# Graph attention with eight heads on one core: the value product visited once per step, and a head's output summed on ScalarE and GpSimd in the second head group

## What is computed

```python
h = jnp.maximum(_layernorm(x, axis=-1), 0.0)
adj = jnp.maximum(adj, eye)
q, k, v = (einsum('nd,hdk->hnk', h, W) for W in (Wqs, Wks, Wvs))
scores = einsum('hqk,hmk->hqm', q, k) * 64 ** -0.5
scores = scores + 0.01 * eye - 1e16 * (1.0 - adj)
att = softmax(scores, axis=-1)
return x + einsum('hqm,hmk,hko->qo', att, v, Wo)
```

## Time and profile before

| | |
|---|---|
| runs of the kernel | 2651.34 us median of 3 (2651.14 to 2653.06) |
| the profiled execution | 2648.64 us, of which 2647.1 us from its first to its last instruction |
| PE | busy 98% of the span, clock 0.998 of full speed |
| DVE | busy 85% |
| ACT | busy 70% |
| POOL | busy 48%, half of it issuing the moves |

### The profile page before, as it was taken

One profiled execution on the slowest core, in us unless ns is written; L12 is line 12 of the kernel. 1 busy time (PEld: TensorE's weight loads), 2 busy tenths in 40 slices (PEclk: granted clock), 3 DMA queues, 4 the chain that ended last, 5 costly groups with the idle time before them and its releaser, 6 DMA issues.

```text
span 2647.1 us, 58489 instructions
## 1 busy us (share of the span) xinstructions
PE 2597.6 (98%) x17344; PEld 1897.9 (72%) x17344; DVE 2254.0 (85%) x3833; ACT 1844.7 (70%) x3041; POOL 1281.6 (48%) x2424
## 2 busy tenths in 40 slices
PE   8999999999999999999999999999999999999997
PEld 5777777777777777777767777777777777777775
DVE  8888888888888888888858888888888888888885
ACT  5677676776767767777747677777767777776764
POOL 3355655556566555665403444434343444434343
PEclk9999999999999999999999999999999999999999
DMA  7467777677778767787645556666555666655563
GB/s 187 125 166 169 182 177 181 171 166 173 174 177 192 171 167 166 172 181 176 162 137 126 138 144 152 165 145 161 144 138 145 153 161 147 162 141 140 144 145 105
DMA packets 268608, 419.06 MB, mean 158 GB/s; under 512 B 100544, under 2 KB 121536, under 8 KB 268544
## 3 DMA queue, kind: packets, MB, share of 16 engines
q1 hardware_dynamic: 178784, 231.24, 34.3%
q0 software_dynamic: 89760, 187.05, 30.8%
HBM read 136.84 MB, written 46.27 MB: 69 GB/s over the span
## 4 chain that ended last, share of the span: by engine, by line
PE 85%; SPq 5%; DMA 4%; DVE 3%; issue 2%; POOL 0%; ACT 0%; DVEq 0%; POOLq 0%; ACTq 0%
PE psS L511 31%; PE psO L548 16%; PE psT L524 15%; PE psO L534 15%; SPq L301 5%; DMA S<-S 3%; PE psS L181 2%; DVE S L777 2%; PE psP L496 2%; PE psP L165 2%; PE psP L484 1%; DVE S L798 1%; PE psO L484 1%; DMA rden_scratch<-rden 0%; POOL S L362 0%
## 5 line engine op out<-in xcount | busy, mean ns | idle before, releaser
L362 POOL DMA_DIRECT2D S<-S x2048 | 1005.6, 499 | 1098.2 <-DVE S L798 1047.3
L777 DVE CUSTOM_DVE_ANT_0 S<-psS,B 128x1024 f32<-128x1024 f32 x1024 | 1227.5, 1218 | 217.8 <-PE psS L511 149.2
L662 ACT ACTIVATE S<-S,negm 128x1024 f32<-128x1024 f32 (+1 forms) x768 | 1095.9, 1428 | 43.9 <-DVE negm L784 43.5
L669 ACT ACTIVATE PT<-psT 128x512 f32<-128x512 f32 x1024 | 594.8, 595 | 254.0 <-PE psT L524 235.3
L511 PE MATMUL psS<-K,QH 128*128 128x512 f32 x2048 | 724.8, 435 | 16.9 <-DVE mx L777 16.4
L511 PE MATMUL psS<-K,QL 128*128 128x512 f32 x2048 | 640.5, 394 | 0.0
L798 DVE STREAM_TRANSPOSE S<-S 128x2048 f32<-128x2048 f32 x256 | 590.4, 2306 | 38.7 <-PE psO L548 35.2
L524 PEld LDWEIGHTS psT<-ident,S 128*128 128x128 f32 x4096 | 480.5, 140 | 185.9 <-issue 73.1
L524 PE MATMUL psT<-ident,S 128*128 128x128 f32 x4096 | 606.6, 276 | 2.9 <-ACT PT L669 2.9
L534 PE MATMUL psO<-PT,V 128*64 128x256 f32 x4096 | 492.1, 382 | 0.0
L548 PE MATMUL psO<-S,V 128*64 128x256 f32 x4096 | 470.3, 382 | 2.4 <-DMA S<-S 2.4
(11 more groups left out here) (51 smaller groups left out, 968.4 us busy)
## 6 DMA issues: line engine op xcount, KB each, us to landing
S<-S SPq DMA_DIRECT2D x2048, 64.0 KB, 3.0
S<-S POOLq DMA_DIRECT2D x2048, 64.0 KB, 2.8
B<-in_adj POOLq DMA_DIRECT2D x128, 256.0 KB, 6.8
bias_scratch<-B SPq DMA_DIRECT2D x64, 512.0 KB, 3.8
B<-bias_scratch SPq DMA_DIRECT2D x128, 256.0 KB, 4.3
hq<-hT_scratch SPq DMA_DIRECT2D x32, 256.0 KB, 4.8
RB<-rden_scratch SPq DMA_DIRECT2D x128, 64.0 KB, 3.4
S<-in_x SPq DMA_DIRECT2D x8, 512.0 KB, 4.6
```

The lines of the kernel that those rows point to most:

```text
L362: pool.dma_start(dst, src).then_inc(late_sent[q][half], 16)
L662: nc.scalar.activation(part, part, ACT.Exp, bias=negm[:, h % 2, q:q + 1], accum_out=sums[:, h % 2, q, e:e + 1]).then_inc(probs_ready, 1)
L669: nc.scalar.activation(PT[:, s % RING, :], psT[s % 2][:, :], ACT.Copy).then_inc(pt_act, 1)
L777: nc.vector.tensor_tensor_reduce(out=part, in0=psS[j % 2][:, :], in1=B[:, q, k * SLOT:(k + 1) * SLOT], scale=SCALE, scalar=LOWEST, op0=ALU ...
```

## The change

- On PE all eight slots are transposed before any value product. The three runs of value products (slots 0 to 3, late keys, slots 4 to 7), which stood in two places of a step, follow each other in one place, after score 7 of the next step and ahead of score 0 of the step after it.
- So that eight slots can wait for their product, slots 4 to 7 are taken into a part of `S` that has already been transposed (`PT_of`).
- On DVE the row's end (`row_done`) is cut off from mask 3 and mask 7; the first stands behind mask 4. `denominators` stands ahead of masks 6 and 7, `transpose_late` of q 1 and `add_heads` stand ahead of masks 0 and 1.
- On ACT the exponentials are in another order; the third piece of q 0 comes last in the step, behind the copy of `psO`.
- In group two, ACT copies both halves of `psO` (after a wait for `projected`), and POOL adds and scales them (`sum_and_scale`), behind its moves of the step; DVE's `sum_halves` is used in group one alone.
- POOL waits for other semaphores ahead of the next group's loads.

```diff
+EXP_ORDER = [(0, 0), (0, 1), (1, 0), (1, 1), (0, 2), (1, 2)]
...
+    def PT_of(h, s):
+        if s < RING:
+            return PT[:, s, :]
+        first = (s - RING) * 2 * QW
+        return S[:, h % 2, 0, first:first + 2 * QW]
...
# POOL
+        def sum_and_scale(i, h):
+            rows = slice(h % 2 * KD, (h % 2 + 1) * KD)
+            wait_apart(pool, odd_copied, count(i, h, 1, 1 + START), pool_passed)
+            nc.gpsimd.tensor_tensor(O[rows, :], O[rows, :], Oodd[rows, :], ALU.add).then_inc(o_summed, 1)
+            wait_apart(pool, o_summed, count(i, h, 1, 1 + START), pool_passed)
+            wait_apart(pool, rden_in, count(i, h, 16, 16), pool_passed)
+            own = O[rows, :].rearrange("k (q p) -> k q p", q=QT)
+            nc.gpsimd.tensor_tensor(own, own, RB[rows, :].rearrange("k (p q) -> k q p", q=QT), ALU.mult).then_inc(o_ready, 1)
...
+            if not norm and (prev or h):
+                sum_and_scale(*last_step(i, h))
             if prev and h == 1:
                 store(i - 1)
                 load_base(i)
...
# PE, step
-            for s in range(4):
+            transposes(i, h, 0)
+            transposes(i, h, 1)
+            if nxt:
+                scores(i1, h1, 2)
+            transposes(i, h, 2)
+            if nxt:
+                scores(i1, h1, 3)
+            if nxt2 and h % 2 == 0:
+                query(i2, h2, h2 == 0, isinstance(i, int) and i == 0 and h == 0)
+            for s in (3, 4):
                 transposes(i, h, s)
                 if nxt:
-                    scores(i1, h1, 2 + s)
+                    scores(i1, h1, s + 1)
+            transposes(i, h, 5)
+            for s in (6, 7):
+                transposes(i, h, s)
+                if nxt:
+                    scores(i1, h1, s)
             for s in range(4):
                 values(i, h, s)
-            for s in range(4, 6):
-                transposes(i, h, s)
-                if nxt:
-                    scores(i1, h1, 2 + s)
-            transposes(i, h, 6)
-            transposes(i, h, 7)
+            values_late(i, h, range(LATE))
+            for s in range(4, TS):
+                values(i, h, s)
             if nxt2:
                 scores(i2, h2, 0)
...
-            values_late(i, h, range(LATE))
-            for s in range(4, TS):
-                values(i, h, s)
...
# ACT, step
+            for s in range(3, 6):
+                take_slot(i, h, s)
+            if nxt:
+                exps(i1, h1, 0, 0)
...
+                exps(i1, h1, 0, 1)
                 exps(i1, h1, 1, 0)
                 exps(i1, h1, 1, 1)
...
+                act.wait_ge(projected, count(i, h, 1, START - h % 2))
+                nc.scalar.activation(Oodd[rows, :], psO[KD:2 * KD, 0:QW], ACT.Copy)
+                nc.scalar.activation(O[rows, :], psO[0:KD, 0:QW], ACT.Copy).then_inc(odd_copied, 1)
+            if nxt:
+                exps(i1, h1, 0, 2)
...
# DVE, step
+                mask(i1, h1, 4)
+                row_done(i1, h1, 0)
+                mask(i1, h1, 5)
+            if prev and norm:
                 sum_halves(*last_step(i, h))
+            denominators(i, h)
             if nxt:
-                mask(i1, h1, 4)
-                mask(i1, h1, 5)
+                mask(i1, h1, 6)
+                mask(i1, h1, 7)
+                row_done(i1, h1, 1)
+                transpose_late(i1, h1, 0, True)
             if nxt2 and h % 2 == 0:
                 query_lo(i2, h2, 0)
                 query_lo(i2, h2, 1)
-            denominators(i, h)
+            if nxt:
+                transpose_late(i1, h1, 1, True)
             if h % 2 and not (isinstance(i, int) and i == 0 and h == 1):
                 add_heads(*((i, 1) if h == 3 else (i - 1, 3)))
-            if nxt:
-                mask(i1, h1, 6)
-                mask(i1, h1, 7)
-            if nxt:
-                transpose_late(i1, h1, 0, True)
             if nxt2:
                 mask(i2, h2, 0)
                 mask(i2, h2, 1)
-            if nxt:
-                transpose_late(i1, h1, 1, True)
```

More of the change, by code:

```diff
@@ L68, in staged_in @@
     return divmod(j - SPT, HALVES)
[L71 to L75, removed]
 def wait_apart(engine, sem, value, passed):
@@ L518, in transposes @@
                 if first_key == 2 * s * P:
-                    pe.wait_ge(probs_ready, count(i, h, QT * NE, NE + e + 1))
+                    pe.wait_ge(probs_ready, count(i, h, QT * NE, max(exps_done(q, e) for q in range(QT))))
             wait_taken(pe, i, h, s - 2)
@@ L567, in step @@
                 values(i, h, s)
[L568 to L573 removed]
+            if not nxt and g + 1 < GROUPS:
+                ahead[g + 1, "PE"](pe)
+            values_late(i, h, range(LATE))
+            for s in range(4, TS):
+                values(i, h, s)
             if nxt2:
@@ L581, in step @@
                 scores(i2, h2, 1)
-            if not nxt and g + 1 < GROUPS:
-                ahead[g + 1, "PE"](pe)
-            values_late(i, h, range(LATE))
-            for s in range(4, TS):
-                values(i, h, s)
-        pe.sem_inc(pt_free, RING)
+        pe.sem_inc(pt_free, TS)
         pe.sem_inc(projected, START)
@@ L667, in take_slot @@
             act.wait_ge(transposed, count(i, h, TS, s + 1))
-            act.wait_ge(pt_free, count(i, h, TS, ring_used(s)))
-            nc.scalar.activation(PT[:, s % RING, :], psT[s % 2][:, :], ACT.Copy).then_inc(pt_act, 1)
+            if s < RING:
+                act.wait_ge(pt_free, count(i, h, TS, s + 1))
+            nc.scalar.activation(PT_of(h, s), psT[s % 2][:, :], ACT.Copy).then_inc(pt_act, 1)
         def step(i, h, nxt, nxt2, prev):
@@ L695, in step @@
                 ahead[g + 1, "ACT"](act)
-            act.wait_ge(pt_free, count(i, h, TS, TS + RING))
+            act.wait_ge(pt_free, count(i, h, TS, TS + TS))
             act.wait_ge(o_ready, count(i, h, 1, START))
-            nc.scalar.activation(Oodd[:, :], psO[KD:2 * KD, 0:QW], ACT.Copy).then_inc(odd_copied, 1)
+            if norm:
+                nc.scalar.activation(Oodd[0:KD, :], psO[KD:2 * KD, 0:QW], ACT.Copy).then_inc(odd_copied, 1)
+            else:
+                act.wait_ge(projected, count(i, h, 1, START - h % 2))
+                rows = slice(h % 2 * KD, (h % 2 + 1) * KD)
+                nc.scalar.activation(Oodd[rows, :], psO[KD:2 * KD, 0:QW], ACT.Copy)
+                nc.scalar.activation(O[rows, :], psO[0:KD, 0:QW], ACT.Copy).then_inc(odd_copied, 1)
+            if nxt:
+                exps(i1, h1, 0, 2)
         if norm:
@@ L809, in sum_halves @@
             dve.wait_ge(odd_copied, count(i, h, 1, 1))
-            nc.vector.tensor_tensor(Oodd[:, :], psO[0:KD, 0:QW], Oodd[:, :], ALU.add).then_inc(o_summed, 1)
+            nc.vector.tensor_tensor(Oodd[0:KD, :], psO[0:KD, 0:QW], Oodd[0:KD, :], ALU.add).then_inc(o_summed, 1)
             dve.wait_ge(o_summed, count(i, h, 1, 1 + START))
@@ L905, in vector_program @@
             ahead[g + 1, "DVE"](dve)
-        sum_halves(PAIRS - 1, GROUP - 1)
+        if norm:
+            sum_halves(PAIRS - 1, GROUP - 1)
         add_heads(PAIRS - 1, GROUP - 1)
```

69 lines of the change are left out of this document (37 added, 32 removed).

## The result

The changed kernel takes **2784.14 us** (median of 4 runs, 2778.86 to 2787.00) against 2651.64 (4 runs, 2651.14 to 2653.06): ratio 1.0505, 95% interval 1.0492 to 1.0518. It is slower, as forecast, but by 132 us instead of 52, and lies above the range. The profiled execution took 2778.86 us.

A forecast was written before the change was run, and what follows sets the result against it. PE was taken as the bound, at 77.27 us a block in group two. Added blocks, 15 x 1.7 + 15 x 2.0, and small terms gave +56 on 2651.3, 2707, lowered to 2703 us; range 2646 to 2737.

The forecast's parts named there:

- The visit saved: PE enters the value products once instead of twice in each of 128 steps: 0.29 us a step, 37 us in all.
- `add_heads`, `store`, the moves: Late add_heads delays POOL's store, so the moves of step (i,2) begin at 1.9 us in the step, 5 us late.
- Group one: Step (i,2): PE's late values wait 3.8 us for moves landing at 15.8; block 80.2 us, 2.0 more than before.
- Group two, the step that failed: Step (i,2) about 22.5 us: mask 5 waits for moves, score 7 at 11.0, PE 2.0 us late; block 79.0, 1.7 more.
- I take 4.5 and 5.5: Landing times in us assumed for the moves of step (i,2), in group two and group one.
- the sum: Adding all terms: blocks of 79.0 us in group two and 80.2 in group one, 56 us more in all, 2707 us.
- shorter landings: The middle of the landing times' bounds lies below those taken, so the forecast was lowered from 2707 to 2703 us.
- ACT behind the projection: Group two: exponentials queue behind ACT's psO copies, which wait for projected; PE waits 0.3 us after each even step, 0.6 a block.
- Small terms: DVE savings and reorderings counted as nothing; POOL's operations 0.75 us each; 1.5 us once at the kernel's end.
- lower bound of group two: With moves landing in 2.8 us, score 7 is 0.3 late and a group two block takes 77.0 us.
- Rivals: First: moves late but hidden, 2636 us, chance 0.14. Second: the visit's gain equals step (i,2)'s cost, 2651 us, 0.06.
- Rival 3: POOL's arithmetic holds up DVE's diagonal fix through a shared read port in group two: 32 us more, 2735 us, chance 0.04.

The follow-up runs named there:

- Version 8: version 2 with sum and scaling of a head's output back on DVE in both groups: 2629.5 us.
- experiments 1 to 3: version 1, version 2, and the kernel before with only add_heads moved behind the transpose of row block 0, ahead of masks 0 and 1: 2730.5 us.
- Version 6: Changed kernel with load_base alone issued behind POOL's moves of step (i,2), wait and store left ahead of them: 2723.5 us.
- version 4: Changed kernel with POOL's wait for add_heads kept at the end of (i,1), but store and load_base issued behind the moves of (i,2): 2712.7 us.
- experiment 7: version 2 with a second buffer of O, so ACT's copies wait for the projection of the pair before the last: 2633.1 us.
- version 2: Changed kernel with add_heads moved back to right behind denominators, ahead of masks 6 and 7: 2644.2 us.
- version 10: version 2 with load_base put directly ahead of the moves of step (i,2), behind the wait for their transpose: 2652.0 us.
- version 1: Changed kernel with POOL's store and load_base moved from the end of step (i,1) to the end of (i,2): 2669.3 us.

## Why the prediction was right in kind and wrong in size

- **The visit saved**: right in kind. Steps that nothing disturbs are 0.22 us shorter (18.42 to 18.19, 20.13 to 19.92), 28 us over 128 steps where I took 0.29 and 37. Version 8, which keeps the visit saved and puts the sum of heads early, is 21 us faster than before.
- **`add_heads`, `store`, the moves**: right. The moves start at 1.6 in the step (forecast 1.9), and experiments 1 to 3 show that this order makes the loss.
- **Group one**: (i,2) is 23.99, forecast "24 in group one", and by the path forecast: POOL's last move lands at 15.7 in the step (mean of 14 blocks; forecast 15.8), and PE's late values wait for it, though only for 18.7 of the 50.3 us that PE idles in the 14 blocks; the rest it has lost before, mostly ahead of scores, where masks were late. (i,3) grows by 0.4 besides, which I had not counted. A block is 2.7 slower, forecast 2.0: 15 x 0.7 = 11 us of the miss.
- **Group two, the step that failed**: "I take 4.5 and 5.5, for the same traffic is there". It isn't. The 4.5 of the earlier trace rows is the landing where `store` and `load_base` had gone out 5 us ahead of the moves; now they go out directly ahead of them, and the moves land in 6.0. I counted the time that it takes to issue the two, not their 512 KB. So mask 4 waits, which I had not thought late, and mask 5 hardly. Step (i,2) became 26.51 instead of 22.5. The landing alone doesn't explain it: with 6.0 the sum gives a block of 80.5, and 83.32 was measured. Of the 2.8 left the clock is some 1.6 (next point); the rest, by difference, is mask 4, whose wait for q 0's first half I had put at nothing. Version 6, whose moves do land in 4.3, has 22.26, near the 22.5, and score 7 at 10.9 in the step where the sum has 11.0; but its moves begin 1.0 earlier than in the sum, and what was late was mask 4 and not mask 5, so part of this agreement is luck.
- **The clock, absent from the sum**: behind mask 4's wait PE idles 3.8 to 4.8 us in each step (i,2) of the 14 blocks, and in each of them the granted clock falls. Over 14 blocks of group two PE is busy 1105.84 us; in version 4, with the same instructions and the clock at 1.00, 1082.99:

```profile
1533.96:2645.56 1111.60, 1082.99 (x7394) 813.66 (x7393) 907.17 (x1484) 807.86 (x1345) 544.36 (x1038) 1.00 0.59 146
```

  That is 22.85/14 = 1.6 us a block of the 3.9 that the bytes cost there; some of it may be waiting that the modelled ends of matmuls hide.
- Together group two is 6.05 a block slower, forecast 1.7: 15 x 4.35 = 65 us of the miss. What is left of the 80 are the 4 us that I had taken off the sum for shorter landings.
- **ACT behind the projection**: right, 0.26 where I had 0.3, by experiment 7.
- **Small terms**: POOL's operations take 0.71 to 0.75 (taken: 0.75). In the lower bound of group two I left out the 0.3 for DVE: 77.3 instead of 77.0, which moves the low end by some 4 us and nothing else.
- **Rivals**: 1 and 2 wanted landings of 3 to 3.5 us, and fall with the 6.0. Rival 3 is real as a mechanism, below, but held up the fix of the diagonal in 4 of 256 cases in the changed kernel, one of them in group two.

Why `load_base` on time costs group one 1.26 us and group two nothing, PE's late values tell. This is their wait in 14 blocks of group one (us, times) and the window of these blocks, for version 2 and then for version 10:

```profile
DMA S<-S: 17.3, 13
185.99:1279.62 1093.63, 1073.91 (x7393) 817.09 (x7392) 953.43 (x1598) 788.63 (x1288) 652.33 (x1178) 1.00 0.73 175
DMA S<-S: 28.3, 14
185.30:1295.66 1110.36, 1080.08 (x7393) 821.19 (x7392) 954.87 (x1598) 788.00 (x1288) 651.09 (x1178) 0.99 0.72 172
```

In group one they wait for moves in nearly every block already, so a later landing goes through whole: 11.0 of the 16.7 us by which the 14 blocks are longer. In the rest PE is busy, 6.2 us more, at a mean clock of 0.99. In group two the late values wait for no move in either version, so the 256 KB have room.

And why group one hardly gains when the bytes go: the same windows of versions 4 and 6, to be read against the first one of the changed kernel.

```profile
186.89:1317.91 1131.02, 1088.48 (x7393) 824.01 (x7392) 957.55 (x1598) 788.85 (x1288) 648.93 (x1175) 0.99 0.70 169
185.95:1327.29 1141.34, 1093.29 (x7393) 827.34 (x7392) 959.56 (x1598) 787.75 (x1288) 649.92 (x1178) 0.98 0.70 168
```

PE's idle time, the length less the busy time, is 50.3 us in the changed kernel, 42.5 in version 4 and 48.1 in version 6: the bytes did cost group one some 0.55 us of waiting a block. But PE is busy 5.3 and 10.1 us longer, at a clock of 0.99 and 0.98, which takes back most of it in version 4 and more than all of it in version 6.

What stays open: why the clock falls in group one of versions 4 and 6 and hardly in the changed kernel's, where PE idles more in all; how the 2.8 us of group two divide between mask 4's wait and the clock, for which I have only the difference in PE's busy time; and version 1's wait for the denominators.

## What to carry to other kernels

An instruction whose result nobody needs soon may still not be moved freely: look at which other engine waits for it, and at what stands behind that wait in the other engine's program. When transfers become late, take their landing time from a stretch with the same bytes ahead of them, since here the same 64 KB took 2.9, 4.3 or 6.0 us. And a long stall of PE can have a second price: the clock fell behind 4.06 us of idling, and not in the same step of version 6, where PE idled 1.17.

## What the runs showed of the hardware

An addition on DVE with both operands in SBUF can stand still while POOL computes. In version 6 the fix of the diagonal, 0.29 us otherwise, took 2.46; DVE's and POOL's timelines there:

```profile
563.89 2.46 DVE L824 TENSOR_TENSOR S<-S,diag 128x128 f32 x1
```

```profile
564.14 2.06 POOL L354 TENSOR_SCALAR B<-B 128x1024 bf16<-128x1024 bf16 x2
```

It ends at 566.35, 0.15 after POOL's two conversions (566.20). The Trainium skill, "SBUF — State Buffer", section "Who interferes with whom", has the rule: a VectorE instruction with two inputs in SBUF and a GpSimd one that reads SBUF share a port, and one waits for the whole of the other. The trace agrees, with one thing more: DVE waited for both of POOL's instructions, and here, by the records, they began 0.25 us after it. By the order of these starts POOL would have been the one to wait; no run here explains that. The pair that rival 3 named does it too, in group two of version 6:

```profile
1887.55 0.82 DVE L824 TENSOR_TENSOR S<-S,diag 128x128 f32 x1
```

```profile
1887.49 0.73 POOL L386 TENSOR_TENSOR O<-O,Oodd 64x256 f32<-64x256 f32 x1
```

The fix ends at 1888.37, 0.15 after POOL's sum. In version 6 the fix took over 0.35 us in 25 of 256 cases, 11 of them in group two; in the kernel before in none.
